# Transposes by 32x32 squares and SBUF transfers, stationary-weight router and mixer output, tokens as 4p+t

## What is computed

```
x = x + 0.5 * ffn(layernorm(x))
x = x + mixer(layernorm(x))
x = x + 0.5 * ffn(layernorm(x))

ffn(h):   scores = sigmoid(h @ router_w.T); 2 of 4 groups of experts by scores + bias,
          then 4 of the 32 experts; weights = 2.5 * chosen scores / their sum
          sum over experts of weight * down(silu(gate(h)) * up(h)) + shared expert
mixer(h): sigmoid gate * (5-tap centred convolution over time), then y[t] = a*y[t-1] + u[t],
          res = h + y @ W_out.T, layernorm(res) * ln_w + ln_b
```

## Time and profile before

| | |
|---|---|
| runs | 674.28 us median (674.2 to 674.43, 3 runs) |
| profiled execution, its own time | 674.34 us |
| its span (first to last instruction) | 672.5 us |
| TensorE's granted clock, mean | 0.997 |
| busy: TensorE, VectorE, ScalarE, GpSimd | 98%, 82%, 62%, 66% |
| SyncE's DMAs, chief kinds | x_ln 8, x_res 8, out 9, wT store 15, wb load 60 |

### The profile page before, as it was taken

One profiled execution on the slowest core, in us unless ns is written; L12 is line 12 of the kernel. 1 busy time (PEld: TensorE's weight loads), 2 busy tenths in 40 slices (PEclk: granted clock), 3 DMA queues, 4 the chain that ended last, 5 costly groups with the idle time before them and its releaser, 6 DMA issues. The chain is left out here.

```text
span 672.5 us, 9867 instructions
## 1 busy us (share of the span) xinstructions
PE 656.8 (98%) x3048; PEld 530.6 (79%) x3048; DVE 550.6 (82%) x1545; ACT 419.4 (62%) x800; POOL 444.9 (66%) x444
## 2 busy tenths in 40 slices
PE   7899999999999999999999999999999999999997
PEld 6687888888888887888888888888878778777785
DVE  5888889988978888889779798688989967967765
ACT  3656576675576656766567765767576576655554
POOL 1256558775676776766767766868676777676654
PEclk9899999999999999999999999999999999999999
DMA  8100100100001000010001000000000000100001
GB/s 215 53 17 20 32 0 21 33 20 17 4 18 32 20 17 21 1 44 9 16 21 31 21 1 24 13 17 20 17 9 13 1 20 3 34 1 17 20 1 31
DMA packets 24853, 15.55 MB, mean 23 GB/s; under 512 B 6592, under 2 KB 21856, under 8 KB 24800
## 3 DMA queue, kind: packets, MB, share of 16 engines
q1 hardware_dynamic: 24224, 14.90, 7.7%
q10 hardware_dynamic: 576, 0.02, 0.1%
HBM read 11.83 MB, written 3.08 MB: 22 GB/s over the span
## 5 line engine op out<-in xcount | busy, mean ns | idle before, releaser
L564 POOL TENSOR_TENSOR hid_lo<-hid,hid_hi 128x512 fp32r<-128x512 f32 x270 | 348.6, 1295 | 192.3 <-ACT hid_hi L671 191.9
L820 DVE TENSOR_TENSOR weighted<-gate_ps,wb 128x512 f32<-128x512 f32 x256 | 175.1, 684 | 68.6 <-ACT gate_ps L663 63.6
L663 ACT ACTIVATE gate_ps<-gate_ps 128x512 f32<-128x512 f32 x256 | 148.7, 581 | 122.4 <-PE gate_ps L1109 119.3
L671 ACT ACTIVATE hid_hi<-hid 128x512 fp32r<-128x512 f32 x272 | 170.5, 627 | 61.0 <-DVE hid L833 56.6
L833 DVE TENSOR_TENSOR hid<-weighted,up_ps 128x512 f32<-128x512 f32 x256 | 174.4, 681 | 8.4 <-POOL hid_lo L564 0.5
L1177 PE MATMUL down_ps<-hid_lo,wt_hi 128*128 128x512 f32 x272 | 107.9, 397 | 0.2 <-DVE hid_lo L841 0.2
L1174 PE MATMUL down_ps<-hid_hi,wt_hi 128*128 128x512 f32 x272 | 107.7, 396 | 0.0
L1175 PE MATMUL down_ps<-hid_hi,wt_lo 128*128 128x512 f32 x272 | 107.5, 395 | 0.0
L1107 PE MATMUL gate_ps<-xT_hi,wt_hi 128*128 128x512 f32 x170 | 71.9, 423 | 0.0
L1107 PE MATMUL up_ps<-xT_hi,wt_hi 128*128 128x512 f32 x170 | 68.4, 402 | 2.3 <-DVE hid L833 2.3
L1108 PE MATMUL gate_ps<-xT_lo,wt_hi 128*128 128x512 f32 x170 | 67.4, 397 | 0.0
(11 more groups left out here) (194 smaller groups left out, 1104.0 us busy)
## 6 DMA issues: line engine op xcount, KB each, us to landing
wb<-wT_hbm SPq DMA_DIRECT2D x60, 64.0 KB, 2.1
x_ln<-in_L_attn_x SPq DMA_DIRECT2D x8, 256.0 KB, 3.1
x_res<-in_L_attn_x SPq DMA_DIRECT2D x8, 256.0 KB, 2.8
out_x<-x SPq DMA_DIRECT2D x7, 256.0 KB, 2.3
raw_gate<-in_L_ffn_gate_w SPq DMA_DIRECT2D x4, 256.0 KB, 4.7
raw_up<-in_L_ffn_up_w SPq DMA_DIRECT2D x4, 256.0 KB, 5.0
raw_down<-in_L_ffn_down_w SPq DMA_DIRECT2D x4, 256.0 KB, 5.2
wT_hbm<-wT SPq DMA_DIRECT2D x15, 64.0 KB, 1.5
```

Of the source, the lines that this page charges most:

```text
L564: nc.gpsimd.tensor_tensor(hid_lo[s][:, :], hid[s][:, :], hid_hi[s][:, :].bitcast(F32), ALU.subtract)\
L663: nc.scalar.activation(bank[:, :] if j else silu_sb[:, :], bank[:, :], ACT.Silu).then_inc(silu_done, 1)
L671: nc.scalar.activation(hid_hi[s][:, :], hid[s][:, :], ACT.Copy).then_inc(hid_hi_done, 1)
L820: V.tensor_tensor(weighted[j % 2][:, :], gate_ps[n % BANKS][:, :], wb[u % 2][:, :], ALU.mult)\
```

## The change

Tokens get the place 4p + t in a block, so that a partition holds four neighbouring tokens. For most blocks the transposes leave TensorE: VectorE transposes the sixteen 32x32 squares of each 128x128 tile in one instruction (`shuffle_norm`, `shuffle_ffn`, `shuffle_mix`), and sixteen SBUF-to-SBUF DMAs on SyncE's queue bring the squares to their partitions (`move_norm`, `move_ffn`, `move_mix`). Readers are ScalarE (`xT_high`) and GpSimd (`xT_low_moved`, `first_ffn_sum`, `mixer_sum`). The router and the mixer output of these blocks use the weights as the stationary operand and 512 columns of tokens (three products). The router's weights stand four times side by side; ScalarE copies four squares of its output (`spread_logits`), VectorE turns them. The routing weights are turned by VectorE and go from SBUF to `wb` in sixteen DMAs, with no way through HBM. The tables of slots are rewritten, and SyncE follows them slot by slot. The first and the last units keep more of the old form.

```diff
+QUAD = 32
+QUADS = P // QUAD
+MOVE = QUADS * QUADS * 16
+MOVED_NORM = {1: range(2, NBLK), 2: range(1, NBLK - 2), 4: range(1, 5)}
+MOVED_FFN = range(1, NBLK - 1)
+MOVED_MIX = range(1, 5)
+SPREAD = {1: range(2, NBLK), 4: range(1, NBLK - 1)}
...
-    x_blk = x.rearrange("a s d -> (a s) d").rearrange("(n t p) d -> n p t d", t=TT, p=P)
+    x_blk = x.rearrange("a s d -> (a s) d").rearrange("(n p t) d -> n p t d", t=TT, p=P)
...
-        ADD = {"copy ffn 1": 1, "transpose ffn 1": 4, "add ffn 1": 8.5}
-        PROJECT = {"stats 2": 1.5, "meanvar 2": 2, "norm 2": 2, "normalise 2": 3, "transpose 2": 9, "xT high 2": 9,
-                   "xT low 2": 9.5, "mixer gate": 10, "tanh gate": 10, "mixer value": 12, "copy value": 12,
-                   "add ln_b": 16}
-        PREPARE = {"transpose 1": 0, "xT high 1": 1, "xT low 1": 1, "router 1": 2, "silu logits 1": 3,
-                   "route 1": even(2, 12), "weights 1": 13}
-        MIXER = {"conv": (0, 0, 0, 0, 0.5, 1.5), "y high": 5, "y low": 5, "mixer out": 9, "mixer sum": 12.5,
-                 "stats 3": 13}
-        ROUTE4 = {"transpose 4": 0, "xT high 4": 0, "xT low 4": 0.5, "router 4": 3, "silu logits 4": 3,
-                  "route 4": even(2.5, 12.5), "weights 4": 13}
-        NEXT = {"stats 1": 13.5, "meanvar 1": 15, "norm 1": 14, "normalise 1": 16}
+        ADD = {"copy ffn 1": 1, "shuffle ffn 1": 3.5, "sum ffn 1": 7, "next x_res": 8}
+        PROJECT = {"stats 2": 0.5, "meanvar 2": 1.5, "norm 2": 3, "normalise 2": 5, "shuffle 2": 7, "xT high 2": 10,
+                   "low 2": 10, "mixer gate": 12, "tanh gate": 12, "mixer value": 14, "copy value": 14,
+                   "add ln_b": 13}
+        NORM4 = {"normalise 3": 3, "scale 3": 4, "x2": 6, "stats 4": 8.5, "meanvar 4": 10, "norm 4": 10,
+                 "normalise 4": 12, "shuffle 4": 14}
+        PREPARE = {"xT high 1": 0, "low 1": 0, "router 1": 2, "spread logits 1": 2, "shuffle logits 1": 3,
+                   "silu logits 1": 5, "route 1": even(4, 14), "weights 1": 14.5}
+        MIXER = {"conv": (0, 0.5, 1, 2, 3, 4.5), "y high": 6, "y low": 6, "mixer out": 8, "shuffle mixer": 9.5,
+                 "sum mixer": 12, "stats 3": 13, "meanvar 3": 14.5, "norm 3": 15}
+        ROUTE4 = {"xT high 4": 0, "low 4": 0, "router 4": 2, "spread logits 4": 3, "shuffle logits 4": 3.5,
+                  "silu logits 4": 5, "route 4": even(4.5, 14.5), "weights 4": 15}
+        NEXT = {"norm 1": 0, "normalise 1": 1, "next x_ln": 3, "shuffle 1": 11}
...
             [
-                ({"stats 1": 14, "meanvar 1": 14, "norm 1": 14, "normalise 1": 16}, 2),
+                ({"stats 1": 11, "meanvar 1": 12, "norm 1": 12, "normalise 1": 13, "next x_ln": 14.5,
+                  "shuffle 1": 14.5}, 2),
...
+                ({"stats 1": 11, "meanvar 1": 12.5, "norm 1": 12, "normalise 1": 14, "next x_ln": 15.5,
+                  "shuffle 1": 15.5}, 3),
...
+            def move_norm(k, b):
+                n = b - MOVED_NORM[k][0]
+                sp.wait_ge(x_shuffled[k], n + 1)
+                sp.wait_ge(xT_lo_done[k], b)
+                for src in range(QUADS):
+                    for dst in range(QUADS):
+                        sp.dma_start(moved_x[k][QUAD * dst:QUAD * dst + QUAD, P * src:P * src + P],
+                                     shuffled_x[k][QUAD * src:QUAD * src + QUAD, P * dst:P * dst + P])\
+                          .then_inc(x_moved[k], 16)
...
             def broadcast_weights(k, b):
                 u = ORDER.index((k, b))
-                sp.wait_ge(wT_done[k], b + 1 if k == 4 else b)
-                if u > 1:
-                    sp.wait_ge(wb_loaded[(u - 1) % 2], u // 2 * 64)
-                sp.dma_start(wT_hbm.rearrange("e (t p) -> (e t) p", t=TT), wT[k][:, :]).then_inc(wT_stored, 16)
-                sp.wait_ge(wT_stored, u * 16)
+                sp.wait_ge(w_shuffled[k], b + 1 if k == 4 else b)
                 if u > 1:
                     sp.wait_ge(weighted_done, (u - 1) * NPAIR)
-                for n in range(SPLIT):
-                    sp.dma_start(wb[u % 2][n:P:SPLIT, :], wT_hbm).then_inc(wb_loaded[u % 2], 16)
+                for src in range(QUADS):
+                    for n in range(SPLIT):
+                        sp.dma_start(wb[u % 2][n:P:SPLIT, P * src:P * src + P],
+                                     wS[k][QUAD * src:QUAD * src + QUAD, :]).then_inc(wb_loaded[u % 2], 16)
...
+            def xT_low_moved(k, b):
+                pool.wait_ge(xT_hi_done[k], b + 1)
+                nc.gpsimd.tensor_tensor(lo_of(k, b), moved_x[k], hi_of(k, b).bitcast(F32), ALU.subtract)\
+                  .then_inc(xT_lo_done[k], 1)
+
+            def first_ffn_sum(b):
+                pool.wait_ge(ffn_moved, (b - MOVED_FFN[0] + 1) * MOVE)
+                pool.wait_ge(x_res_loaded, b * 16 + 16)
+                nc.gpsimd.tensor_tensor(by_dim(x1[b % 2][:, :, :]), by_token(moved_ffn), by_dim(x_res[:, :, :]),
+                                        ALU.add).then_inc(ffn_added[1], 1)
...
             def xT_high(k, b):
-                act.wait_ge(xn_transposed[k], b + 1)
-                nc.scalar.activation(hi_of(k, b), side[:, :], ACT.Copy).then_inc(xT_hi_done[k], 1)
+                if b in MOVED_NORM[k]:
+                    act.wait_ge(x_moved[k], (b - MOVED_NORM[k][0] + 1) * MOVE)
...
+                    nc.scalar.activation(hi_of(k, b), moved_x[k], ACT.Copy).then_inc(xT_hi_done[k], 1)
...
+            def spread_logits(k, b):
+                act.wait_ge(logits_made[k], b - SPREAD[k][0] + 1)
+                act.wait_ge(logits_ready[k], b)
+                for n in range(QUADS):
+                    rows = slice(QUAD * n, QUAD * n + QUAD)
+                    last = nc.scalar.activation(spread[k][rows, :], side[rows, P * n:P * n + P], ACT.Copy)
+                last.then_inc(logits_spread[k], 1)
...
+            def shuffle_norm(k, b):
+                n = b - MOVED_NORM[k][0]
+                dve.wait_ge(ln_normed[k], b + 1)
+                if n > 0:
+                    dve.wait_ge(x_moved[k], n * MOVE)
+                V.transpose(shuffled_x[k].rearrange("p (b r t) -> p t b r", b=QUADS, t=TT),
+                            by_dim(normed[k][:, :, :])).then_inc(x_shuffled[k], 1)
...
             def router(k, b):
                 pe.wait_ge(xT_lo_done[k], b + 1)
                 w_hi, w_lo = wt_hi[:, WROUTER, 0:E], wt_lo[:, WROUTER, 0:E]
+                if b in SPREAD[k]:
+                    product(side[:, :], wt_hi[:, WROUTER, :], hi_of(k, b), lo_of(k, b), wt_lo[:, WROUTER, :],
+                            True, True).then_inc(logits_made[k], 1)
+                    return
...
-            def transpose_route(k, b):
-                pe.wait_ge(route[k], b * ROUTE + ROUTE)
-                nc.tensor.transpose(side[:, 0:P], w_tok[:, :, :].rearrange("p e t -> p (e t)"), ident[:, :])\
-                  .then_inc(route_transposed[k], 1)
...
             def mixer_out(b):
+                if b in MOVED_MIX:
+                    product(side[:, :], wt_hi[:, WOUT, :], y_hi[:, :], y_lo[:, :], wt_lo[:, WOUT, :],
+                            True, True).then_inc(mix_out_ready, 1)
+                    return
```

More of the change, by code:

```diff
@@ L374, in macaron_kernel @@
                   "route 4": even(2.5, 12.5), "weights 4": 15}, 0),
[L375 to L378, removed]
+                ({"conv": (0, 0, 0, 0.5, 1.5, 2.5), "y high": 3, "y low": 3, "mixer out": 6, "shuffle mixer": 7.5,
+                  "sum mixer": 10, "stats 3": 12, "meanvar 3": 13, "norm 3": 14}, 1),
+                ({"copy ffn 1": 1, "shuffle ffn 1": 3.5, "sum ffn 1": 6, "next x_res": 7}, 2),
+                ({"stats 1": 11.5, "meanvar 1": 12.5, "norm 1": 12, "normalise 1": 14, "next x_ln": 15,
+                  "shuffle 1": 15.5}, 4),
             ],
@@ L387, in macaron_kernel @@
                   "meanvar 4": 15.5, "norm 4": 14, "normalise 4": 16}, 5),
[1 row of a table removed]
[L389 to L390 removed]
+                ({"xT high 4": 0, "low 4": 0, "router 4": 2, "spread logits 4": 2, "shuffle logits 4": 3,
+                  "silu logits 4": 4, "route 4": even(3.5, 13.5), "weights 4": 14}, 4),
+                ({"copy ffn 4": 3, "transpose ffn 4": 4, "halve ffn": 6, "add ffn 4": 5, "store": 7}, 3),
                 ({"stats 2": 0, "meanvar 2": 0.5, "norm 2": 0, "normalise 2": 9, "transpose 2": 10, "xT high 2": 10,
@@ L445, in macaron_kernel, with xn_count @@
         LOGITS_READ = 2
+        def xn_count(k, b):
+            return sum(i not in MOVED_NORM[k] for i in range(b + 1))
         MIX = K + 1
@@ L589, in unit @@
                 for j in range(NT):
+                    for n in (1, 2, 4):
+                        for b in due(steps, f"low {n}", j):
+                            xT_low_moved(n, b)
+                    for b in due(steps, "sum ffn 1", j):
+                        first_ffn_sum(b)
+                    for b in due(steps, "sum mixer", j):
+                        mixer_sum(b)
                     for b in due(steps, "norm 3", j):
```

(15 more changed lines are left out.)

252 lines of the change are left out of this document (161 added, 91 removed), and 3 rows, old and new, of the table END.

## The result

The changed kernel takes 902.71 us (median of 4 runs, 901.89 to 904.86), the kernel before 674.24 (4 runs): 1.340 times as long, interval 1.338 to 1.342. The forecast was 752 us, 651 to 790; the direction was right, and the loss, 228 us, three times what was worked out. The profiled execution's span is 903.1 us.

The account below looks back on a forecast made before the run. TensorE, busy 98% of the span, was taken as the bound. 674.3 us minus 23.1 spared on TensorE plus 101 of stalls from SyncE's queue (62 steady units, 34 beginning, 5 end) gave 752 us, range 651 to 790.

Parts of the forecast that it names:

- The bound and the direction: Whole kernel: TensorE, busy 98% of the span, sets the pace; SyncE's late queue makes it slower, likeliest 752 us, chance 0.66.
- I take 0.47 for moves (same size) and for the broadcasts, whose two neighbours disagree, the middle, 0.55: SyncE's queue: us per DMA issue, so 16 issues hold it 7.5 us for a move, 8.8 for a broadcast.
- The prediction's own deadlines: Steady units: when moved data is due against when usable; late by 2.7 and 8.7 us (second-FFN), 5.4 (first-FFN).
- 75.3: Us for a steady pair, one second-FFN and one first-FFN unit, forecast without stalls.
- The forecast's worst rival: SyncE's queue: every issue costs the broadcast's price, 0.63 us; stalls of 173 us, 824 us in all; chance 0.03.
- GpSimd waits for it some 2 us, within its slack of three tiles: First-FFN units, mixer move: GpSimd's wait for the moved mixer output was claimed to fit its slack.
- Token layout 4p+t: [...] 0, covered by slack on ScalarE: Whole kernel: strided writes of unmoved copies cost 0, at worst a doubled 0.6 us for nine copies.
- none becomes the bound, TensorE covers them: Work added to other engines stays hidden: VectorE near 33 of some 37.7 us a unit, GpSimd near 30.
- TensorE's saving of 23.1 us: TensorE spared: transposes 9.2 us, routers 7.7 (0.64 each), mixer outputs 2.6, transposes of routing weights 3.6.
- The square transposes: VectorE: 25 transposes of 128x512 at 0.69 us each, bounds 0.35 and 1.4, adding 0 on the path.
- The clock, 0 in the sum and 17 at the top: TensorE at half speed for 3.4 us after some ten stalls of 5 to 11 us: 0 to 17 us lost.
- Begin 34 and end 5: Stalls in us from late moves and broadcasts in the first four units, and from broadcasts alone in the last units.

Follow-up runs that it names:

- four issues: The changed kernel with only 4 of the 16 DMAs of every move and every broadcast of weights, the other 12 left out: 708.6 us.
- last two rows of the table: The changed kernel with 4 of 16 DMAs per move and broadcast, 708.6 us; the same with contiguous reads in unmoved routers, mixer outputs and FFN transposes, 698.4 us.
- the best version here: The kernel before with stationary routers in three steady first-FFN units, and all 15 blocks' routing weights by VectorE's squares, four stores and four loads: 672.68 us, ratio 0.9979.
- its trial: The kernel before with trial DMAs of six kinds on SyncE's queue, behind the broadcast of six middle units: 674.1 us.
- that trial: The changed kernel with 40 added products of 32 columns ahead of routers, mixer gates and second-FFN units' tile 3 gate, in units 1 to 11: 962.8 us.

## Why the prediction was right and wrong

- **The bound and the direction: right.** TensorE had no gap, so each stall lengthened the run. Two kinds of stall stand where the prediction put them: the mixer gate of second-FFN units, and the gate of tile 3 of steady units (with the router before it in first-FFN units).
- **"I take 0.47 for moves (same size) and for the broadcasts, whose two neighbours disagree, the middle, 0.55": the step that failed.** Both cost 0.63. The row nearest in size had HBM on one side, and size does not set the price. The prediction's own deadlines worked with 0.633 and a landing of 1.8 give stalls of 7.9, 12.3 and 11.6 us, 31.8 a pair where it had 16.8; TensorE's gaps in the measured pair are 28.5 us (the other 9.5 us by which it exceeds 75.3 are longer work, 8.5 of them from the lower clock). So the mechanism was right, and one term, mis-sized by a third, doubled the stalls: the slack is spent first, and every further 0.1 us of price counts 16 times a move. The Trainium skill (page DMA: Bandwidth & Descriptors, section Anatomy of one DMA) states some 50 ns of dispatch for the path on which GpSimd issues; on SyncE's queue the runs show 0.63 us.
- **How much of the miss that is.** The forecast's worst rival had this price, stalls of 173 us for 101, and 824 us, with a chance of 0.03. So the price makes 72 of the 151 us between 752 and 903. Another 58 are there with four issues too (708.6 for 651); the bullets below name what was found of their causes. Some 21 us are left open.
- **"GpSimd waits for it some 2 us, within its slack of three tiles": wrong at the measured price.** The mixer's move kept GpSimd 5.35 us, and VectorE and TensorE behind it: 5.98, 4.94 and 5.98 us of TensorE in the three steady first-FFN units. What is lost here is no longer lost at the next tile 3, which waited 5.2 to 5.9 us where the deadlines, at the right price, give 11.6; so the sum came out nearly right and the place did not.
- **"Token layout 4p+t: [...] 0, covered by slack on ScalarE": wrong.** It looked at writes by ScalarE and not at TensorE's stationary reads, which are on the path: 38 us where all are strided, 8 to 10 in what the change leaves of them.
- **"none becomes the bound, TensorE covers them": wrong where work is bunched.** By sums it held (VectorE 36.3 us of work in a unit of 59.6). But steps in slots meet by order, not by sums: the quarter copies came at 0.27 as forecast, and second-FFN units with them lost more than the router saved. With four issues a steady pair takes 80.2 us, 4.9 more than the 75.3; 3.0 of that are TensorE's gaps behind VectorE's tiles. In the third unit it is GpSimd that is late for ScalarE's norm.
- **TensorE's saving of 23.1 us: smaller, and given back.** A router saves 0.47 us of the forecast's 0.64 where nobody is late; router and routing weights together 0.67 of 0.88. The saving of the transposes and of the mixer output was not measured alone.
- **The square transposes: mis-sized within their bounds.** 1.09 to 1.11 us for 0.69 in 21 of the 25 (bounds 0.35 and 1.4); the mixer's four, which read PSUM, took 0.71.
- **The clock, 0 in the sum and 17 at the top: right in the sum, for another reason.** Ten short drops were expected, 17 us lost at most; 198 us came, 55 us lost. In the steady units most of that did not reach the end: 20 us of it won back left them as long as they were.
- **Begin 34 and end 5: too small.** Against the kernel before, the first four units lost 64.7 us and the last four 22.9; 46.7 and 15.2 of that go with the number of issues, 3.2 and 5.0 with the strided reads and the change of chip (last two rows of the table). Most of what is left at the beginning is the third unit, whose norm waits for GpSimd.

## What to carry to other kernels

Price a DMA issue by the kind of transfer (which memories, which partitions), from a row of that very kind; if there is none, take the dearest neighbour, because a queue that is late multiplies the error by its count. When a layout changes, follow it into every reader, TensorE's stationary loads first. Work taken from a full engine pays only in a stage where the engines that get it have room in that slot; of a forecast 23 us, the best version here kept 1.7 us, no more than the spread between chips.

## What the runs showed of the hardware

Issues back to back on SyncE's queue stand 0.46 us apart with HBM on one side and 0.63 between two places in SBUF, there from 16 to 256 KB; loads from HBM to every fourth partition stood 0.63 apart too. The first store of its trial, right behind the broadcast's last issue, took 0.58 us, the other fifteen 0.42, and so did the first load: by these rows an issue's duration goes with the kind of the one ahead of it. A copy that writes 128x512 at a step of four floats takes ScalarE 1.09 us for 0.60, VectorE's difference 1.09 for 0.69 (groups of the changed kernel):

```profile
L814 ACT ACTIVATE xT_hi<-side 128x512 fp32r<-128x512 f32 x6 | 6.5, 1089 | 1.0 <-PE side L1358 0.6 <-PE side L1500 0.3
```

And TensorE's granted clock can fall while it works: during 40 products of 32 columns without a gap it went from 1.00 to a mean of 0.72 and was at 0.50, the lower of its two levels (1.2 of 2.4 GHz), through the next 40 (windows of that trial, columns as above):

```profile
517.30:523.50 6.20, 6.20 (x28) 5.02 (x27) 2.24 (x7) 2.75 (x5) 5.13 (x5) 1.00 0.11 26
523.60:529.60 6.00, 6.00 (x42) 6.00 (x40) 0.00 (x0) 1.09 (x2) 0.00 (x0) 0.72 0.11 26
533.10:541.70 8.60, 8.59 (x41) 8.59 (x41) 0.00 (x0) 0.00 (x0) 0.30 (x1) 0.50 0.00 0
```
